# Attention over units of two batches and half of the queries in place of units of one batch

## The reference

```python
q, k, v = (split_heads(hidden_states @ W.T + b) for W, b in ...)      # B=4, H=16, N=1024, D=8
buckets = _relative_position_bucket(N, N)                             # 40 buckets of the distance j - i
pos_bias = transpose(rel_embed[buckets], (2, 0, 1))                   # H, N, N
gates = sigmoid((ghs @ gru_W.T + gru_b).reshape(B, H, N, 2, 4).sum(-1))
gate_out = gates[..., 0:1] * (gates[..., 1:2] * gru_const - 1.0) + 2.0
scores = einsum('bhid,bhjd->bhij', q, k) / sqrt(D) + gate_out * pos_bias[None]
out = einsum('bhij,bhjd->bhid', softmax(scores), v)
```

## Time and profile before

| what | us |
|---|---|
| median of 3 runs | 2294.89 (2293.07 to 2296.41) |
| the profiled execution's own time | 2297.82 |
| its span | 2296.0 |
| the phase of the change, from its first product to its last division | 124.75 to 1022.6 |
| PE busy over the span | 2004.4 (87%) |
| DVE busy over the span | 1625.2 (71%) |
| ACT busy over the span | 1348.2 (59%) |

### The profile page before, as it was taken

The page is one execution under the profiler, slowest core; times in us unless marked ns, Lnnn a source line. Parts: engine busy times, 40 slices in busy tenths (PEclk is TensorE's granted clock), DMA queues, the critical chain, the costliest instruction groups (busy, mean ns, idle before and its releaser), DMA issues. The chain is left out here.

```text
span 2296.0 us, 56479 instructions
## 1 busy us (share of the span) xinstructions
PE 2004.4 (87%) x17787; PEld 1018.4 (44%) x17787; DVE 1625.2 (71%) x3441; ACT 1348.2 (59%) x2150; POOL 1099.2 (48%) x987
## 2 busy tenths in 40 slices
PE   5569999999999999975799759999999999998576
PEld 3324444444444444444344214444444444444355
DVE  4778888888888888767565776666666666664696
ACT  2226666666666666542455437777777777777121
POOL 1132322232223222414355317877877787877464
PEclk8869999999999999986899979999999999999787
DMA  5521111122112211100000460011111011100000
GB/s 133 156 62 51 55 54 49 50 55 53 49 50 55 53 49 51 47 11 1 1 1 0 154 194 29 29 41 28 41 28 42 28 42 28 42 14 1 0 14 23
DMA packets 127050, 107.03 MB, mean 47 GB/s; under 512 B 39636, under 2 KB 102724, under 8 KB 126956
## 3 DMA queue, kind: packets, MB, share of 16 engines
q1 hardware_dynamic: 124640, 103.37, 16.5%
q10 hardware_dynamic: 2316, 2.64, 0.4%
HBM read 76.01 MB, written 29.53 MB: 46 GB/s over the span
## 5 line engine op out<-in xcount | busy, mean ns | idle before, releaser
L1048 DVE TENSOR_REDUCE b_mx<-psum 128x1 f32<-128x512 f32 x1024 | 663.8, 686 | 145.7 <-PE psum L867 82.6
L1032 ACT ACTIVATE b_prob<-psum 128x1024 f32<-128x1024 f32 x512 | 524.3, 1024 | 319.8 <-PE psum L899 319.7
L1806 POOL TENSOR_TENSOR f_plo<-f_prob,f_phi 128x512 f16<-128x512 f32 x512 | 587.6, 1158 | 169.4 <-ACT f_phi L1931 144.2
L1949 DVE TENSOR_REDUCE f_mx<-psum 128x1 f32<-128x512 f32 x512 | 328.7, 683 | 169.0 <-PE psum L1826 167.9
L1930 ACT ACTIVATE f_prob<-psum 128x512 f32<-128x512 f32 x512 | 308.1, 602 | 158.1 <-PE psum L1837 153.4
L947 PE MATMUL psum<-b_prob,b_v 128*32 128x256 f32 x4096 | 328.3, 392 | 1.6 <-ACT b_prob L1032 0.5
L1931 ACT ACTIVATE f_phi<-psum 128x512 f16<-128x512 f32 x512 | 306.4, 598 | 0.0
L805 POOL COPY b_v<-v 128x64 f32 x64 | 15.2, 238 | 596.1 <-PE psum L947 595.8
L899 PE MATMUL psum<-b_diag,b_toep 128*128 128x79 f16 (+1 forms) x4224 | 267.4, 208 | 0.0
L899 PEld LDWEIGHTS psum<-b_diag,b_toep 128*128 128x128 f16 x4224 | 235.9, 99 | 9.1 <-issue 2.6
L808 POOL TENSOR_TENSOR b_diag<-flip,grev 128x1024 f16<-128x1024 f16 x128 | 239.8, 1895 | 0.0
(11 more groups left out here) (312 smaller groups left out, 3407.4 us busy)
## 6 DMA issues: line engine op xcount, KB each, us to landing
d_qk<-e_qk SPq DMA_DIRECT2D x64, 256.0 KB, 2.6
b_toep<-d_line SPq DMA_DIRECT2D x128, 64.0 KB
f_qa<-d_qk SPq DMA_DIRECT2D x64, 128.0 KB, 2.8
f_ka<-d_qk SPq DMA_DIRECT2D x64, 128.0 KB, 2.9
b_q<-d_q SPq DMA_DIRECT2D x128, 54.0 KB
d_k<-a_qk SPq DMA_DIRECT2D x48, 128.0 KB, 2.3
b_toep<-d_line SPq DMA_DIRECT2D x128, 32.0 KB
b_q<-b_m SPq DMA_DIRECT2D x256, 1.0 KB
```

The lines of the kernel that those rows point to most:

```text
L1032: nc.scalar.activation(prob[:, t % 4, :].rearrange("p (a n) -> p a n", a=2), ps[:, EXP + 2 * (t % 2):EXP + 2 * (t % 2) + 2, :], ACT.Exp).t ...
L1048: nc.vector.tensor_reduce(mx[:, b, t, half:half + 1], ps[:, bank, :], AX.X, ALU.max).then_inc(s.max_read, 1)
L1806: nc.gpsimd.tensor_tensor(plo[:, t % 4, at], prob[:, t % 4, at], phi[:, t % 4, at], ALU.subtract).then_inc(s.plo_ready, 1)
L1949: nc.vector.tensor_reduce(mx[:, b, t, half:half + 1], ps[:, MAX + half, :], AX.X, ALU.max).then_inc(s.max_read, 1)
```

## The change

- A **unit** is now two batches and half of the queries: `idx // 2` chooses the pair of batches, `idx % 2` (hf) the quarters of queries, hf and 2 + hf. There are again 64 units of 8 steps, each step still with 1024 columns of scores: for i in 0, 1 a bank with one quarter of both batches.
- The near products of the exponentials take both batches in one instruction (2x79 or 2x128 columns). A step has 0, 3 or 6 of them; before it had 6 or 9. The key tiles are taken in `ORDER`, in which steps with 6 and with 3 alternate.
- The far products of the exponentials are cut by quarter and batch: 36 of mostly 256 columns in a unit, before 22 of mostly 512. They are written in turn over the row groups, between those for the maxima. The waits for the two ring banks now stand ahead of the exponentials' far products.
- LEAD 12 becomes 13; `values` runs two steps behind (LAG) instead of one.
- `join_max` moves from step 3 to 2, `turn_m` from 4 to 3, `turn_o` from 2 to 4 and with it `divide_o` from 3 to 5; it now takes two multiplications. `turn_m` takes two products.
- `toep` and `diag` are separate for maxima and exponentials, so POOL makes six scaled identities for two batches, before four.
- Loads join the two batches: 14 DMAs for a pair of batches, before 32. `store_m` still takes four.

The diff, cut to its core:

```diff
-        LEAD = 12
+        LEAD = 13
+        LAG = 2
+        QUARTER = N // 4
+        ORDER = ((0, 2, 1, 3, 4, 6, 5, 7), (2, 0, 3, 1, 6, 4, 7, 5))
...
+        toep_max = sb("b_toep_max", [P, 2, 3 * P], F16)
+        toep_exp = sb("b_toep_exp", [P, 2, 2, 3 * P], F16)
+        diag_max = g.combT[:, :].rearrange("p (s t e) -> p s t e", s=SLOTS, t=TB)
+        diag_exp = g.x16[:, :, :].rearrange("p a t -> p (a t)").rearrange("p (s x t e) -> p s x t e", s=SLOTS, x=2, t=TB)
...
-        OUT_STEP, M_STEP = 2, 4
+        OUT_STEP, M_STEP = 4, 3
+        JOIN_STEP = 2 * TB - 1 - LEAD
         ring = []
         for t in range(TB):
             ring += [(t, 0), (t, 1)]
+            if t == M_STEP:
+                ring.append("m")
             if t == OUT_STEP:
                 ring.append("o")
-            if t == M_STEP:
-                ring.append("m")
...
+        def query_tile(idx, n):
+
+            bb, i, y = n // 4, n // 2 % 2, n % 2
+            return 2 * (idx // 2) + bb, 4 * i + 2 * (idx % 2) + y
...
                 with sp.Fori(0, H0 - 1) as k:
-                    for b in range(B):
-                        store_m(k + (b + 1) // 4, (b + 1) % 4)
-                        load(k + 1, b)
...
+                    store_m(k, 1)
+                    load_exp(k, 1)
+                    load_max(k + 1, 0)
+                    store_m(k, 2)
+                    store_m(k, 3)
+                    load_exp(k + 1, 0)
+                    load_max(k + 1, 1)
+                    store_m(k + 1, 0)
...
+                def for_max(h, pair):
+                    for half in range(2):
+                        pool.wait_ge(s.max_psum[half], done(TB * (4 * (h - 1) + 2 * pair + 1) + TB - 1))
+                    for b in (2 * pair, 2 * pair + 1):
+                        nc.gpsimd.tensor_tensor(diag_max[:, b, :, :], flips, gates(h, b, 0), ALU.mult).then_inc(s.diag_max_ready, 1)
...
-                    return [x for x in near if half * BANK <= x[1] * P < (half + 1) * BANK]
...
+                    return [x for x in near if x[1] // 2 == 2 * i + hf]
+
+                def exp_far(bb, i, idx, pos, left):
+
+                    pair, hf = idx // 2, idx % 2
+                    b, t, bank = 2 * pair + bb, ORDER[hf][pos], EXP + 2 * (pos % 2) + i
+                    c0 = (2 * i + hf) * QUARTER
+                    c1 = c0 + QUARTER
                     mid = min(max(t * P, c0), c1)
...
+                def exp_near(i, idx, pos):
...
+                    both = ps[:, bank, :].rearrange("p (b q) -> p b q", b=2)
                     last = None
-                    for blk, qt, x, y in exp_near_of(t, half):
+                    for blk, qt, x, y in exp_near_of(t, i, hf):
                         for tp, dp in ((0, 0), (0, 1), (1, 0)):
-                            at = qt * P - c0
-                            last = nc.tensor.matmul(ps[:, bank, at + x:at + y], toep[:, b, tp, blk * P:(blk + 1) * P], diag[:, b, dp, qt, x:y],
+                            at = qt % 2 * P
+                            last = nc.tensor.matmul(both[:, :, at + x:at + y], toep_exp[:, pair, tp, blk * P:(blk + 1) * P],
+                                                    diag_exp[:, 2 * pair:2 * pair + 2, dp, qt, x:y],
                                                     start=False, stop=(tp, dp) == (1, 0), skip_group_check=True)
...
+                    if ahead:
+                        at = [ring.index((pos, half)) for half in range(2)]
                         for half in range(2):
-                            last = exp_far(b, t, half, left) or last
+                            bank_free(h, idx, at[half])
+                        banks = [RING + x % BANKS for x in at]
+                    last, fars = [None, None], []
+                    for step in range(4):
+                        for i in range(2):
+                            last[i] = exp_far(step // 2, i, idx, pos, step % 2 == 1) or last[i]
+                        if ahead and step < 2:
+                            fars += max_fars(im, nm, banks, step == 1)
...
+                    for bb in range(2):
+                        tiles = slice((2 * (b // 2) + bb) * TB, (2 * (b // 2) + bb + 1) * TB)
+                        out = g.attn[:, tiles, bass.ds(h * D0, D0)].rearrange("p (i f y) d -> p f y i d", i=2, f=2)[:, b % 2]
+                        ins = nc.vector.tensor_tensor(out, o[:, :, :, bb, 0:D0], r[:, :, :, bb:bb + 1].to_broadcast([P, 2, 2, D0]), ALU.mult)
...
-                        if t == 3 and left >= 1:
+                        if t == JOIN_STEP and left >= 1:
                             join_max(*after(1))
```

More of the change, by code:

```diff
@@ L837, in bank_free @@
                         pe.wait_ge(s.o_ready, done(item - 1))
+                    elif ring[at] == "m" and isinstance(item, int) and item == NI - 1:
+                        pe.wait_ge(s.max_read, done(2 * TB * NI - 1))
                     elif ring[at] == "m":
@@ L886, in exp_far @@
                         return
-                    rows = slice(half * GROUP, (half + 1) * GROUP)
-                    both = c0 < mid < c1
-                    return nc.tensor.matmul(ps[:, bank, x - c0:y - c0], ks[b][int(not left)][rows, t * P:(t + 1) * P], qs[b][rows, x:y],
-                                            start=not (left and both), stop=not exp_near_of(t, half), skip_group_check=True)
-                def exp_near(b, t, half):
-                    bank, c0 = EXP + 2 * (t % 2) + half, half * BANK
+                    rows = slice(i * GROUP, (i + 1) * GROUP)
@@ new lines, in exp_far @@
+                    opens = bb == 0 and not (left and c0 < mid < c1)
+                    at = bb * QUARTER - c0
+                    return nc.tensor.matmul(ps[:, bank, at + x:at + y], ks[b][int(not left)][rows, t * P:(t + 1) * P], qs[b][rows, x:y],
+                                            start=opens, stop=not exp_near_of(t, i, hf), skip_group_check=True)
+                def exp_near(i, idx, pos):
+                    pair, hf = idx // 2, idx % 2
+                    t, bank = ORDER[hf][pos], EXP + 2 * (pos % 2) + i
+                    both = ps[:, bank, :].rearrange("p (b q) -> p b q", b=2)
@@ L915, in maxima, with max_fars, max_nears @@
+                def max_fars(idx, n, banks, right):
+                    b, t = query_tile(idx, n)
+                    return [max_far(b, t, half, banks[half], right) for half in range(2)]
+                def max_nears(idx, n, banks, fars):
+                    b, t = query_tile(idx, n)
                     for half in range(2):
@@ L995, in item_steps @@
                             turn_o(*before, at)
-                        if t == M_STEP and left >= 1:
-                            at = ring.index("m")
-                            bank_free(h, b, at)
-                            turn_m(*after, at)
                 items(pe, item_steps)
-                values(H0 - 1, B - 1, TB - 1)
+                for t in range(TB - LAG, TB):
+                    values(H0 - 1, B - 1, t)
                 turn_o(H0 - 1, B - 1, ring.index("o"))
```

241 lines of the change are left out of this document (135 added, 106 removed).

## The result

| | before | change |
|---|---|---|
| median, us | 2295.65 (2293.07 to 2305.23, 4 runs) | 2416.05 (2414.36 to 2417.92, 4 runs) |
| span of the profiled execution | 2296.0 | 2412.6 |
| ratio of the medians | | 1.0502, 95% interval 1.0465 to 1.0538 |

What follows compares the result with a forecast made beforehand. PE was taken as the bound, with 12.23 us of work and 1.26 of waits an item; 0.23 more over 62 units (14.3) plus 2.7 at the end made 17.0, so 2312 us, range 2288 to 2332.

Steps and rivals of the forecast that it cites:

- At nothing: POOL: POOL's six products of 1.90 us for two units, 11.4 of 27 us, run ahead of need and cost nothing.
- The clock: PE's granted clock, read as 1.00 (2.4 GHz) in the earlier profile, was taken as given.
- Near products joined: On PE, 66 near products become 33 a unit with the same columns, saving 0.08 us a unit.
- Rival A: An instruction costs more than its columns, so joined near products take as long as one half: 2276 us, chance 0.07.
- Far products cut: On PE, 14 more far products a unit with the same columns cost 0.03 us a unit; the stage stays 0.33.
- rival C: Cutting far products costs 0.03 to 0.06 us a step, passed on through DVE: 2327 to 2343 us, chance 0.12.
- The waits, step by step: PE's waits in a unit, nearly all for banks DVE has still to read, sum to 1.48 us against 1.26 before.
- B: The waits go, since join and division stand apart and DVE's lag is absorbed: 2245 us, chance 0.13.
- D: The forecast waits are 0.2 us too long, so the change nearly cancels out: 2295 to 2299 us, chance 0.10.
- the two new waits: PE waits for banks in steps 4 and 6 of a unit, 0.60 and 0.58 us.
- The ends: The last divisions come later, +2.7 us at the end of the phase; effects at the start sum to 0.
- DMAs at nothing: Loading with 14 DMAs in place of 32 was taken to cost or save nothing.

Runs made afterwards that it cites:

- the held version: The change, with one wait added so POOL starts the exponentials' products only when the join is through: 2328.91 us, ratio 1.0106 to the kernel before.
- the order: The change, with POOL waiting for the join and the tiles reordered so heavy steps stand in steps 2 to 5: 2283.65 us, ratio 0.9933.
- the pieces: The change, with no wait added on POOL, each of POOL's products for the exponentials cut into four: 2344.79 us, ratio 1.0192.

## Why the prediction was wrong

- **At nothing: POOL.** This is the step that failed. "SP and POOL run ahead of need" asked only whether PE waits for POOL's result. It did not ask what POOL's 11.4 us of products in 27 lie beside, now that the join comes a step earlier. Their price is 87 us by the held version, 90 by the phases of the two traces: per pair 1.75 of stop and 1.32 of clock, 3.07 x 32 = 98, less 5 by which the held version takes longer at the end of the phase, and less 1.3 for the first pair; the few that remain are within what two sets of runs differ. In the kernel before the join begins 5.5 us after POOL's block does (486.74 to 492.20), and the block is over after 3.9; in the change it begins 1.5 us after it (305.22 to 306.70), and the block lasts 11.5. By these rows the new distance alone would have met a block of two products, and the longer block alone a join at the old distance. No run separates them.
- **The clock.** The forecast took 1.00 as given because the earlier trace rows had it. PE stood still 1.27 and 0.92 us within one step, and the clock fell, in every pair but the first. The stop costs its length, and where the clock falls behind it three quarters as much again. What decides between the two, no run shows.
- **Near products joined:** right. The forecast had heavy and light stages of 0.63 and 0.30, the trace has 0.63 and 0.30; joining saved 0.05 a unit where 0.08 was taken. Rival A is out: taken apart, 132 more products a head cost 0.05 a unit. So is an overhead of some 60 cycles on top of the columns, as the prediction read the Trainium skill (TensorEngine Tiling (Array Packing), Instruction Overhead). What that section says of a single column, that it takes as long as 60, is not touched by this, since the products here have 79 columns and more, and it fits the idle products of 2 columns: 12 cost 0.38 a unit, 0.032 each, the time of 76 columns. Whether the product or its load of weights sets that, no run separates.
- **Far products cut:** right, 0.33 in all steps; rival C is out.
- **The waits, step by step:** right in kind and nearly in size. Steps 3 to 5 of an undisturbed unit take 2.07, 2.03 and 1.94, forecast about 2.0 each; the unit takes 13.74 there. In the held version 13.82 stand against 13.72: 0.10 more, of which waits of some 0.08 in light steps are a part. Over the phase that is +20 where the sum had +14. Rivals B and D are out. That the two new waits come from light steps with nothing behind which to hide a read is borne out by the order, which takes 0.75 a unit off with the same products.
- **The ends:** +2.7 was too small. From the first exponential of the 61st unit to the last division the held version takes 71.7 us where the kernel before took 64.4: +7.3. The last joins meet POOL's long instructions; PE's wait there grew from 2.75 to 7.34 us, again the same mechanism. The start, which the sum had at 0, is 1.8 longer (25.3 from the first product to the first exponential, before 23.5).
- **DMAs at nothing:** right; PE waits 26.5 us for the loads at the start, 27.45 before, and for none in a unit.

So without the collision the phase is 28.6 us longer than before in the traces (1.8 at the start, 19.5 in 60 units, 7.3 at the end), against 17.0 in the sum. By the medians it is 24.4. What stays open: why the start is longer, what decides whether the clock falls behind a stop, and why the loop of the kernel before has its instructions fetched again in some heads and not in others.

## What to carry to other kernels

An engine with time to spare still takes part in the schedule if its instructions can hold up another's, as POOL's did DVE's here: whenever a small two-input operation or a cast on DVE sits in a chain that TensorE waits for, look up what POOL runs at that moment, before and after every move, and let POOL's instructions be short or start behind it. In a group of instructions, a mean far above the shortest instance is the sign; here even one long instance at the edge of a phase, 3.16 in place of 0.17 us, would have pointed to the mechanism. Only after such a stop is gone can a reordering be judged: here one change measured +5% and, with one wait, an order and shorter pieces on POOL, -1.2%.

## What the runs showed of the hardware

- A cast of 8 elements with a single input in SBUF is held by a POOL instruction as the subtraction is (1.43 us, and 3.16 in the kernel before, in place of 0.17); a reduction with one input is not (0.17 beside a product). By the Trainium skill (SBUF — State Buffer, Who interferes with whom) a cast can enter a mode that takes both ports, where its operands allow it, and a reduction cannot; the rows agree.
- DVE is let in between two POOL instructions that follow each other without a gap (0.53 us in the pieces), 0.03 us after the first of them ends.
- PE stops 3.1 to 5.8 us at every turn of a loop that has 76 or more products above the 676 a head of the change (11%), and the clock drops behind it: 7.8 us a turn, 109 in all, with 132 more. In each head with a stop the instruction queue moves nine packets of 16 KB; between 340 and 960 us of the version with 12 idle products a unit, which has no stop, it moves none. With 72 more, some turns stop and most don't. A kernel near that length pays for its next few instructions with this and not with their own time.
